# Decoder block on one core: fourteen experts' weights split by GpSimd in the routed stage instead of in the cross-attention, attention scores issued one by one on alternating array halves

## The chip, the core and the metric

One core of a Trainium2 chip. Its engines run their own programs side by side and meet at semaphores: PE (TensorE, matrix products into PSUM), DVE (VectorE), ACT (ScalarE), POOL (GpSimd), and SP (SyncE), which issues DMAs. POOL and ACT issue DMAs as well. The metric is the device time of one launch in microseconds, the median of several runs.

## What is computed

One pre-norm decoder layer on x of (8, 256, 512), with self-attention, cross-attention to a context of the same shape, and a mixture of experts:

```python
x = x + attn(layernorm(x), w_qkv, w_out)                 # 16 heads of 32, causal
x = x + xattn(layernorm(x), ctx, ctx, encoding, Wq, bq, Wk, bk, Wv, bv, Wm, bm)
x = x + moe(layernorm(x), Wg, W1, W3, W2, Ws1, Ws3, Ws2)

# xattn: the 256 positions are channels, the 512 features are the sequence
q, k = rotary(Wq x + bq), rotary(Wk c + bk);  v = Wv c + bv      # 16 heads of 16
scores = einsum('bdhn,bdhm->bhnm', q, k) / sqrt(16)
out = Wm einsum('bhnm,bdhm->bdhn', softmax(scores), v) + bm

# moe: 16 experts of 352 hidden units, 4 of them for each token, and 2 shared ones
h = silu(einsum('td,eid->eti', xt, W1)) * einsum('td,eid->eti', xt, W3)
y = einsum('etd,te->td', einsum('eti,edi->etd', h, W2), combine)
```

## The kernel before

Products of f32 data are made of f16 pairs: a value is split into a high part (the value rounded to f16) and a low part (what is left, rounded to f16), and a product is three f16 matmuls, high x high, high x low and low x high (`split_product`). So every operand has to be split once: the high part by ACT or POOL, the low part by a subtraction on POOL or DVE.

The stages run one after the other: self-attention, cross-attention, then routing with the first shared expert, the routed experts, and last the combination with the second shared expert.

**Cross-attention** (`cross_attention`). It handles eight batches in a pipeline of turns, t = -2 to 8. In turn t the attention of batch t is done (`attend`), the row maxima of batch t+1 (`maxima`), and the projections of batch t+2 (`projects`); pieces of batches t+3 and t-1 are prepared and finished (`pairs`, `ends`). A turn has 16 quads, and every engine's program is written out as a loop over them, so the tests such as `qd in (1, 3, 7, 9)` are the schedule. In a quad PE makes four score tiles of 128x512 (`ca_sc`, in `scores`) whose maxima DVE takes (`maximum`, `ca_mx`), four transposed ones for the next quad (`ca_st`, in `transposed_scores`) that ACT exponentiates (`exponent`, `ca_pt`), and it weighs the values with them (`weigh_values`, `ca_pv`). A score tile has 48 or 49 rows of contraction, and the heads lie in partitions 0 to 63 or 64 to 127, so a tile uses one half of the array's rows. `ca_sc` and `ca_st` have three PSUM banks each (`RING = 3`). One more bank, `ca_proj`, is shared by the projections, the values, the turned maxima and the output; `USERS` lists who has it in which order.

Between the scores, DVE does `swap` and `add` of the rotary embedding, `turn_weighed`, `invert`, `divide` (`ca_quot`) and `turn_back` (`ca_yf`) for each of four groups of heads, `residual`, `keep_values` and `normalise`; ACT does `out` (takes a projection out of PSUM), `high_part`, `y_high_part`, `x_high_part`, `keep_maxima`; POOL does `roll` and the low parts; SP does `spill` and `stack` (the rotated q and k go through DRAM into their stacked form), `load_rows` and `load_context`.

The experts' weights are split here too. From quad 4 on each attending turn has 12 pieces of 704 or 768 columns, two experts' worth: SP loads a piece (`load_piece`), ACT makes the high part (`split_piece`), POOL the low part (`low_piece`), SP stores the pair to DRAM (`store_piece`, `we_pairs`). After eight turns `we_pairs` holds all 16 experts.

**Routed experts** (`routed_experts`). Tokens have been sorted by expert into tiles of 128 rows; PE works through 74 tiles. For a tile it makes the two hidden products (`re_ab`, 24 matmuls), transposes the f16 pair of the hidden values (`re_ht_ps`, `turn_hidden`, which waits for `h_low`), and makes the output (`re_yp`, 9 matmuls, in `output`, which counts `y_done`). The hidden values pass through ACT (`re_gate`), DVE (`re_hf`), ACT (`re_hp`, high part, L1542) and DVE (`re_hp`, low part, L1567, which signals `h_low`). PE's order is `hidden` of tile n+1, `turn_hidden` of n, second half of n+1, `output` of n. Weights have two slots. POOL waits until the last tile of an expert is done and loads the next pair from `we_pairs` into that slot with one DMA of 2176 KB. At the start POOL also loads and splits the second shared expert's weights (`jobs`, L1466 and L1468).

## Time and profile before

| | us |
|---|---|
| median of 3 runs (1991.07 to 1993.84) | 1992.2 |
| the profiled execution: its own time | 1993.37 |
| its span in the trace | 1991.8 |
| cross-attention in it, 481.6 to 1217.0 | 735.4 |
| routed experts in it, 1400.0 to 1856.8 | 456.8 |
| busy in the whole span: PE, DVE, ACT, POOL | 1502.9, 1059.7, 694.4, 575.4 |

How to read what follows. A row of the busy times has a stretch (from and to, in us from the start of the span), its length, then for PE, PE's weight loads (PEld), DVE, ACT and POOL the busy time with the count of instructions, then the granted clock of PE as a share of 2.4 GHz, the share of the DMA engines, and GB/s. A row of the timeline has start and length in us, engine, line, operation, output <- inputs, shapes and count, and in brackets the idle time before it and what ended it. A row of the waits says who waited for whom: total, times, longest. Matmul rows have a pipeline tail in their length: neighbours overlap. Each load of an expert's pair is 2176 KB, 9.2 us from issue to landing at the median; the second shared expert's weights are as large, in two DMAs.

### The profile page before, as it was taken

To read this page: it belongs to the slowest core of one execution; us is meant where nothing else is said; L and a number is where in the kernel's file an instruction comes from. 1 tells how busy PE (TensorE), PEld (TensorE's weight loads), DVE (VectorE), ACT (ScalarE), POOL (GpSimd) and SP (SyncE) were. 2 spreads that over 40 slices of the span, in tenths; PEclk is the share of its full clock that TensorE was granted. 3 is DMA by queue.
4 is the path that set the end of the run, shared out by engine and by line. 5 is a ranking of instruction groups with operands and counts; after the bars stand their busy time and mean duration, and the time that the engine had idled before them with its cause. 6 is when DMAs were issued, how large, how long until landed. Compare 5 with 4: busy or idle time off the path is not lost. (4 is left out here: it accounts for less than half of the span.)

```text
span 1991.8 us, 28978 instructions
## 1 busy us (share of the span) xinstructions
PE 1502.9 (75%) x9512; PEld 687.2 (35%) x9521; DVE 1059.7 (53%) x1809; ACT 694.4 (35%) x1187; POOL 575.4 (29%) x464
## 2 busy tenths in 40 slices
PE   2778787875266667768677774885699999999957
PEld 1344444442011111112111111532366566666423
DVE  6343434346387777876776726851143333333564
ACT  4322221212116766666766683511011111111211
POOL 3000000002534554554544332467200000000462
PEclk9989898987558989898898886787799999999978
DMA  4252516160423555545644451035555645654564
GB/s 169 72 172 61 182 48 195 36 207 31 116 53 96 159 167 147 174 125 147 181 123 135 154 160 70 1 134 204 182 179 179 176 138 176 181 177 137 140 178 131
DMA packets 212442, 273.45 MB, mean 137 GB/s; under 512 B 91984, under 2 KB 159120, under 8 KB 210064
## 3 DMA queue, kind: packets, MB, share of 16 engines
q1 hardware_dynamic: 188880, 181.68, 32.2%
q0 software_dynamic: 12832, 71.44, 10.3%
q10 hardware_dynamic: 10656, 19.40, 2.6%
q8 instruction: 39, 0.64, 0.1%
q14 instruction: 35, 0.29, 0.1%
HBM read 132.29 MB, written 120.06 MB: 127 GB/s over the span
## 5 line engine op out<-in xcount | busy, mean ns | idle before, releaser
L805 DVE TENSOR_REDUCE ca_mx<-ca_sc 128x1 f32<-128x512 f32 x512 | 331.9, 678 | 165.9 <-PE ca_sc L725 163.6
L77 PE MATMUL re_ab<-re_w,re_xt 128*128 x1800 | 297.6, 316 | 42.5 <-DMA re_w<-we_pairs 38.5
L938 ACT ACTIVATE ca_pt<-ca_st 128x512 f32<-128x512 f32 x512 | 274.9, 590 | 37.5 <-PE ca_st L737 37.1
L737 PE MATMUL ca_st<-ca_qs,ca_ks 49*128 49x512 f16 x512 | 110.2, 426 | 155.6 <-ACT ca_pt L938 155.5
L77 PEld LDWEIGHTS re_ab<-re_w,re_xt 128*128 128x128 f16 x1800 | 174.1, 99 | 141.2 <-issue 44.4
L1003 POOL TENSOR_TENSOR ca_wpair<-ca_wraw,ca_wpair 128x704 f16<-128x704 f32 (+1 forms) x96 | 149.3, 1561 | 65.7 <-ACT ca_wpair L895 65.7
L750 PE MATMUL ca_pv<-ca_pt,ca_va 128*32 128x512 f32 x1024 | 163.1, 701 | 0.9 <-DVE ca_turned L818 0.6
L77 PE MATMUL re_yp<-re_w,re_ht 128*128 (+1 forms) x666 | 156.0, 379 | 0.0
L737 PEld LDWEIGHTS ca_st<-ca_qs,ca_ks 49*128 49x128 f16 x512 | 25.3, 94 | 349.6 <-ACT ca_pt L938 287.6
L725 PE MATMUL ca_sc<-ca_ks,ca_qs 48*128 48x512 f16 x512 | 113.1, 438 | 39.5 <-DVE ca_mx L805 20.6
L478 POOL TENSOR_TENSOR sa_yt<-sa_yf,sa_yt 128x512 f16<-128x512 f32 x16 | 18.5, 1156 | 385.0 <-ACT sa_yt L461 385.0
L77 PE MATMUL sh_ab<-fx_xn,sh_pair 128*128 128x512 f16 (+1 forms) x576 | 126.6, 382 | 3.6 <-PEq L1408 3.4
L1540 ACT ACTIVATE re_gate<-re_ab 128x352 f32<-128x352 f32 x75 | 34.8, 463 | 252.8 <-PE re_ab L77 252.8
L1457 POOL DMA_DIRECT2D re_w<-we_pairs x16 | 8.6, 536 | 371.0 <-PE re_yp L77 354.2
L1565 DVE TENSOR_TENSOR re_hf<-re_ab,re_gate 128x352 f32<-128x352 f32 x75 | 39.3, 524 | 112.1 <-PE re_ab L77 112.1
L1576 DVE COPY re_ht<-re_ht_ps 128x768 f16<-128x768 f16 x74 | 41.3, 557 | 108.1 <-PE re_ht_ps L1499 108.1
L77 PE MATMUL sh_yp<-sh_pair,sh_ht 128*128 128x512 f16 (+1 forms) x288 | 72.2, 412 | 34.5 <-DVE x_sb L1208 34.4
L1608 POOL DMA_INDIRECT co_yg<-slot_outs,fx_index x64 | 69.7, 1090 | 96.7 <-POOLq L1408 61.5
L1542 ACT ACTIVATE re_hp<-re_hf 128x352 f16<-128x352 f32 x75 | 37.2, 496 | 173.2 <-DVE re_hf L1565 173.2
L77 PE MATMUL sa_proj<-sa_xn,sa_w 128*128 x384 | 85.3, 385 | 10.7 <-DVEq L407 10.7
L77 PEld LDWEIGHTS re_yp<-re_w,re_ht 128*128 128x128 f16 (+1 forms) x666 | 65.1, 98 | 69.0
L988 POOL TENSOR_TENSOR ca_tf<-ca_tf,ca_freq 128x512 f32<-128x512 f32 x32 | 40.8, 1276 | 162.0 <-DVE ca_rf L796 162.0
(235 smaller groups left out, 2415.9 us busy)
## 6 DMA issues: line engine op xcount, KB each, us to landing
re_w<-we_pairs POOLq DMA_DIRECT2D x16, 2176.0 KB, 9.2
ca_wraw<-in_we SPq DMA_DIRECT2D x64, 352.0 KB, 3.8
we_pairs<-ca_wpair SPq DMA_DIRECT2D x64, 352.0 KB, 2.9
slot_rows<-sa_zeros SPq DMA_DIRECT2D x12, 1792.0 KB, 16.0
slot_outs<-re_ys ACTq DMA_DIRECT2D x74, 256.0 KB, 2.0
ca_wraw<-in_we SPq DMA_DIRECT2D x32, 384.0 KB, 4.8
we_pairs<-ca_wpair SPq DMA_DIRECT2D x32, 384.0 KB, 2.9
sa_scratch<-sa_qk SPq DMA_DIRECT2D x16, 512.0 KB, 4.5
```

Source lines behind the costliest of these rows:

```text
L77: last = nc.tensor.matmul(out, lhs(a, c), rhs(b, c), start=(c == 0 and n == 0), stop=(c == chunks - 1 and n == len(PRODUCTS) - 1))
L725: nc.tensor.matmul(sc[:, (2 * n + a) % RING, :], qs[rows, c % SLOTS, pair, qt * P:(qt + 1) * P], ks[rows, c % SLOTS, pair, :], start=True, ...
L737: nc.tensor.matmul(st[:, (2 * n + a) % RING, :], ks[rows, b % SLOTS, pair, kt * P:(kt + 1) * P], qs[rows, b % SLOTS, pair, :], start=True, ...
L750: last = nc.tensor.matmul(pv[j * 32:(j + 1) * 32, :], va[:, b % 2, kt, h, :], pt[:, (4 * qd + j) % 8, :], start=(kt == 0), stop=(kt == 3), ...
L805: nc.vector.reduce_max(mx[:, qd // 4, qd % 4, 2 * a + jj:2 * a + jj + 1], sc[:, (2 * n + a) % RING, :], AX.X).then_inc(maxed, 1)
L938: nc.scalar.activation(pt[:, (4 * qd + k) % 8, :], st[:, (2 * n + a) % RING, :], ACT.Exp, scale=SCALE).then_inc(exp_done, 1)
L988: nc.gpsimd.tensor_tensor(tf[:, u, :], tf[:, u, :], freq[:, 0, :], ALU.mult).then_inc(rolled, 1)
L1003: nc.gpsimd.tensor_tensor(wpair[:, m % 2, 1, 0:n], wraw[:, m % 3, 0:n], wpair[:, m % 2, 0, 0:n], ALU.subtract).then_inc(w_low, 1)
L1542: nc.scalar.activation(hp[:, s, 0, :], hf[:, s, :], ACT.Copy).then_inc(h_high, 1)
L1565: nc.vector.tensor_tensor(hf[:, s, :], ab[:, s, 1, 0:I], gate[:, s, :], ALU.mult).then_inc(h_ready, 1)
L1576: nc.vector.tensor_copy(ht[:, s, :, :], ht_ps[:, 0:2 * IC, :]).then_inc(ht_ready, 1)
L1608: nc.gpsimd.indirect_dma_start(out=yg[:, m % RING, :], out_offset=None, in_=slot_outs, in_offset=bass.IndirectOffsetOnAxis(ap=route["index ...
```

## The change

Four things change.

- **Pieces.** Only 12 pieces, those of experts 0 and 1, are still split in the cross-attention, in the turn t = -1, which has no exponentials. `we_pairs` has two experts.
- **Routed stage.** Experts 2 to 15 are loaded raw, as f32, into a buffer of two (`raw_w`). When a slot is free POOL splits the expert itself: one `tensor_copy` and one `tensor_tensor` subtraction over all 4352 columns. `w_ready` takes the place of the DMA's semaphore on PE. At the start both stored pairs, the shared expert's two pieces and two raw experts are all issued at once.
- **Scores.** `scores` and `transposed_scores` issued two matmuls on one wait; `score` and `transposed_score` issue one. Their order by halves of the array is k % 2 for the one and 1 - k % 2 for the other. The order of heads in `weigh_values` and in the layout of Wm follows.
- **Places in the schedule.** Several small steps stand in later quads; `turn_maxima(3, b)` goes from quad 1 to 7.

```diff
-            def scores(c, qd, jj):
-                n, pair, qt = 2 * (QUADS * c + qd) + jj, 2 * (qd // 4) + jj, qd % 4
-                if n >= 1:
-                    pe.wait_ge(maxed, 2 * n - 1)
-                for a in range(2):
...
+            def score(c, qd, k):
+                m, pair, qt = 4 * (QUADS * c + qd) + k, 2 * (qd // 4) + k // 2, qd % 4
+                if m >= RING:
+                    pe.wait_ge(maxed, m - RING + 1)
+                rows = slice(64 * (k % 2), 64 * (k % 2) + ROWS)
...
+            def transposed_score(b, qd, k):
+                if m >= RING:
+                    pe.wait_ge(exp_done, m - RING + 1)
+                a = 1 - k % 2
...
@@ DVE turn
-                    if projects and qd in (1, 3, 7, 9):
-                        swap((1, 3, 7, 9).index(qd), e)
+                    if projects and qd in (2, 4, 8, 10):
+                        swap((2, 4, 8, 10).index(qd), e)
-                    if projects and qd in (2, 5, 8, 11):
+                    if projects and qd in (3, 6, 9, 11):
                         add(...)
-                    if pairs and qd == 10:
+                    if pairs and qd == 11:
                         normalise(j, f)
@@ ACT turn
-                    if attend and qd == 2:
+                    if attend and qd == 8:
                         keep_maxima(3, b)
-                    if projects and qd in (3, 6, 9, 12):
+                    if projects and qd in (5, 7, 11, 12):
                         high_part(...)
-                    if attend and qd in (5, 9, 13):
+                    if attend and qd in (6, 10, 14):
                         y_high_part(qd // 4 - 1, b)
-                    if pairs and qd == 11:
+                    if pairs and qd == 13:
                         x_high_part(j, f)
-                    if attend and qd >= FIRST_PIECE:
-                        split_piece(b, qd - FIRST_PIECE)
+                    if t == -1 and qd >= FIRST_PIECE:
+                        split_piece(qd - FIRST_PIECE)
@@ SP turn
-                    if projects and qd in (4, 6, 10, 12):
+                    if projects and qd in (6, 8, 12, 13):
                         spill(...)
-                    if projects and qd in (5, 7, 11, 13):
+                    if projects and qd in (7, 9, 13, 14):
                         stack(...)
@@ routed experts, POOL
-            with pool.Fori(1, E // 2) as i:
-                for k in range(2):
-                    pool.wait_ge(w_loaded, 32 * i + 16 * k)
-                    pool.wait_ge(y_done, done + 2)
-                    load(2 * i + k, k)
+            for e in range(2, E):
+                done = pool.value_load(route["ends"][0:1, e - 2:e - 1], min_val=0, max_val=TILES)
+                pool.wait_ge(y_done, done + 2)
+                pool.sem_inc(w_free, 1)
+                pool.wait_ge(raw_loaded[e % 2], 16 * (e // 2))
+                nc.gpsimd.tensor_copy(w[:, e % 2, 0, :], raw_w[:, e % 2, :]).then_inc(w_high, 1)
+                pool.wait_ge(w_high, e - 1)
+                nc.gpsimd.tensor_tensor(w[:, e % 2, 1, :], raw_w[:, e % 2, :], w[:, e % 2, 0, :], ALU.subtract
+                                        ).then_inc(w_ready, 1)
+                if e + 2 < E:
+                    pool.wait_ge(w_ready, e + 1)
+                    load_raw(e + 2)
```

What stands in a row on POOL at the routed stage. Before, the loop's body, one expert of two:

```order
312 L1473 ISA [waits re_w_loaded]
313 L1473 TENSOR_LOAD fx_ends
314 L1473 ISA x2
315 L1474 REGISTER_ALU
316 L1457 ISA [waits re_y_done]
317 L1457 DMA re_w<-we_pairs 128x8704
```

With the change, the same place, one expert of fourteen (`re_raw_w` is the f32 buffer):

```order
225 L1477 TENSOR_LOAD fx_ends
226 L1477 ISA x2
227 L1478 REGISTER_ALU
228 L1481 CAST re_w<-re_raw_w 128x4352 [waits re_y_done,re_raw_loaded0]
229 L1483 TENSOR_TENSOR re_w<-re_raw_w,re_w 128x4352 [waits re_w_high]
230 L1460 DMA re_raw_w<-in_we 128x4352 [waits re_w_ready]
```

Between the free slot and ready weights there was a DMA; now there are two POOL instructions, and the DMA stands behind them for an expert two later.

PE in the cross-attention, a quad of a full turn (`ca_st` are the transposed scores, `ca_sc` those for the maxima). Before:

```order
525 L737 MATMUL ca_st<-ca_qs,ca_ks 128x512 [waits ca_exp_done]
526 L737 MATMUL ca_st<-ca_qs,ca_ks 128x512
527 L725 MATMUL ca_sc<-ca_ks,ca_qs 128x512 [waits ca_maxed]
528 L725 MATMUL ca_sc<-ca_ks,ca_qs 128x512
529 L737 MATMUL ca_st<-ca_qs,ca_ks 128x512 [waits ca_exp_done]
530 L737 MATMUL ca_st<-ca_qs,ca_ks 128x512
531 L725 MATMUL ca_sc<-ca_ks,ca_qs 128x512 [waits ca_maxed]
532 L725 MATMUL ca_sc<-ca_ks,ca_qs 128x512
```

With the change:

```order
524 L736 MATMUL ca_st<-ca_qs,ca_ks 128x512 [waits ca_exp_done]
525 L724 MATMUL ca_sc<-ca_ks,ca_qs 128x512 [waits ca_maxed]
526 L736 MATMUL ca_st<-ca_qs,ca_ks 128x512 [waits ca_exp_done]
527 L724 MATMUL ca_sc<-ca_ks,ca_qs 128x512 [waits ca_maxed]
528 L736 MATMUL ca_st<-ca_qs,ca_ks 128x512 [waits ca_exp_done]
529 L724 MATMUL ca_sc<-ca_ks,ca_qs 128x512 [waits ca_maxed]
530 L736 MATMUL ca_st<-ca_qs,ca_ks 128x512 [waits ca_exp_done]
531 L724 MATMUL ca_sc<-ca_ks,ca_qs 128x512 [waits ca_maxed]
```

The same eight matmuls stand in turn instead of in pairs, and each waits for itself.

## Rows read from the trace of the kernel before

**Rows 1.** Busy time by stage (columns as told under the profile above).
```profile
481.60:1217.00 735.40, 486.44 (x2752) 125.67 (x2752) 493.32 (x935) 431.39 (x765) 345.13 (x255) 0.82 0.47 135
...
1400.00:1856.80 456.80, 443.08 (x2910) 267.26 (x2910) 171.31 (x299) 71.98 (x150) 22.34 (x22) 0.98 0.56 169
```

**Rows 2.** The same view, turns of the cross-attention: first, six full, seventh, eighth.
```profile
544.00:603.90 59.90, 37.39 (x130) 10.20 (x130) 49.68 (x91) 12.41 (x19) 18.86 (x15) 0.53 0.21 46
...
603.90:1077.80 473.90, 336.79 (x2044) 87.93 (x2042) 350.28 (x666) 315.41 (x568) 245.01 (x182) 0.90 0.53 151
...
1077.80:1147.40 69.60, 52.04 (x318) 13.33 (x318) 49.52 (x95) 46.17 (x84) 23.21 (x16) 0.88 0.40 127
...
1147.40:1200.00 52.60, 38.33 (x204) 8.10 (x208) 12.15 (x22) 42.19 (x76) 21.61 (x15) 0.80 0.47 149
```

**Rows 3.** Who waited for whom, 759.4 to 838.9: total us, times, longest.
```profile
DVE ca_mx L805 <- PE ca_sc L725: 20.4, 15, 3.3
...
PE ca_st L737 <- ACT ca_pt L938: 20.1, 23, 4.1
...
ACT ca_tf L915 <- PE ca_proj L77: 8.3, 4, 3.2
...
ACT ca_yt L927 <- DVE ca_yf L834: 6.5, 3, 3.2
...
ACT ca_xn L899 <- DVE ca_norm L784: 2.2, 1, 2.2
```

**Rows 4.** Groups of instructions, the same turn: busy us, mean ns, idle before.
```profile
L895 ACT ACTIVATE ca_wpair<-ca_wraw 128x704 f16<-128x704 f32 x8 | 6.2, 780 | 0.0
```

**Rows 5.** Timeline of PE, then DVE, cross-attention: start us, length us, what.
```profile
763.22 0.39 PE L737 MATMUL ca_st<-ca_qs,ca_ks 49*128 49x512 f16 x2 [0.27 <-ACT ca_pt L938]
...
768.70 1.47 PE L77 MATMUL ca_proj<-ca_xn,ca_w 128*128 128x512 f16 x6
...
770.10 1.07 PE L750 MATMUL ca_pv<-ca_pt,ca_va 128*32 128x512 f32 x8
...
767.63 1.89 DVE L805 TENSOR_REDUCE ca_mx<-ca_sc 128x1 f32<-128x512 f32 x3 [0.65 <-PE ca_sc L725]
```

**Rows 6.** Timeline of POOL, routed stage.
```profile
1424.74 2.53 POOL L1466 CAST sh_pair<-sh_raw 128x2816 f16<-128x2816 f32 x1 [13.37 <-DMA sh_raw<-in_we]
...
1427.36 5.52 POOL L1468 TENSOR_TENSOR sh_pair<-sh_raw,sh_pair 128x2816 f16<-128x2816 f32 x1
...
1611.19 0.53 POOL L1457 DMA_DIRECT2D re_w<-we_pairs  x1 [28.78 <-PE re_yp L77]
```

**Rows 7.** Timeline of PE, then of DVE, one tile of the routed stage.
```profile
1608.43 2.11 PE L77 MATMUL re_yp<-re_w,re_ht 128*128 x9
...
1616.23 1.96 PE L77 MATMUL re_ab<-re_w,re_xt 128*128 x12
...
1618.03 0.50 PE L1499 MATMUL re_ht_ps<-ident,re_hp 128*128 128x128 f16 x6
...
1615.65 0.53 DVE L1567 TENSOR_TENSOR re_hp<-re_hf,re_hp 128x352 f16<-128x352 f32 x1 [0.56 <-ACT re_hp L1542]
```

**Rows 8.** DVE beside POOL: DVE, POOL, DVE; durations ns min/median/max of one line.
```profile
1227.96 4.26 DVE L122 TENSOR_SCALAR fx_ln_std<-fx_ln_moments 128x16 f32<-128x16 f32 x1
...
1226.69 5.51 POOL L226 TENSOR_TENSOR sh_pair<-sh_raw,sh_pair 128x2816 f16<-128x2816 f32 x1 [6.04 <-ACT sh_pair L220]
...
1433.73 0.93 DVE L1567 TENSOR_TENSOR re_hp<-re_hf,re_hp 128x352 f16<-128x352 f32 x1 [0.56 <-ACT re_hp L1542]
...
L826 DVE TENSOR_TENSOR ca_quot<-ca_turned,ca_rden x32: 401/408/1878, 624.8 to 1203.9; 128x256 f32<-128x256 f32 x32
```

**Rows 9.** Busy time around an idle stretch; timeline of PE after another.
```profile
154.95:161.15 6.20, 0.00 (x1) 0.01 (x1) 4.18 (x3) 2.53 (x3) 2.30 (x2) 0.77 0.00 0
...
161.15:165.10 3.95, 3.95 (x10) 1.44 (x11) 0.00 (x0) 0.01 (x1) 0.00 (x0) 0.50 0.00 0
...
1425.62 3.70 PE L77 MATMUL re_ab<-re_w,re_xt 128*128 x12 [3.87 <-DMA re_xt<-slot_rows]
```

More of the change, by code:

```diff
@@ L551, in cross_attention @@
     WP = 2 * NP
[L554 to L555 removed]
+    USERS = (("project", 2, 0), ("project", 2, 1), ("out", -1, 0), ("out", -1, 1), ("maxima", 1, 0),
+             ("project", 2, 2), ("maxima", 0, 3), ("project", 2, 3), ("maxima", 1, 1), ("values", 1, 0), ("values", 1, 1),
              ("values", 1, 2), ("maxima", 1, 2), ("values", 1, 3))
@@ L728, in transposed_scores @@
-            def transposed_scores(b, qd, jj):
-                n, pair, kt = 2 * (QUADS * b + qd) + jj, 2 * (qd // 4) + jj, qd % 4
-                if kt == 0 and jj == 0:
-                    pe.wait_ge(row_loaded[qd // 4], 32 * (b + 1))
-                if n >= 1:
-                    pe.wait_ge(exp_done, 2 * n - 1)
-                for a in range(2):
-                    rows = slice(64 * a, 64 * a + ROWS + 1)
-                    nc.tensor.matmul(st[:, (2 * n + a) % RING, :], ks[rows, b % SLOTS, pair, kt * P:(kt + 1) * P],
-                                     qs[rows, b % SLOTS, pair, :], start=True, stop=True).then_inc(st_done[a], 1)
+                if m >= RING:
+                    pe.wait_ge(maxed, m - RING + 1)
@@ L1455, in _, with load_raw @@
         def _(pool):
-            def load(e, slot):
-                pool.dma_start(w[:, slot, :, :], we_pairs[e]).then_inc(w_loaded, 16)
-            load(0, 0)
-            pool.wait_ge(w_loaded, 16)
-            load(1, 1)
+            def load_raw(e):
+                pool.dma_start(raw_w[:, e % 2, :], we_dram[e]).then_inc(raw_loaded[e % 2], 16)
+            for e in range(2):
+                pool.dma_start(w[:, e, :, :], we_pairs[e]).then_inc(pairs_loaded[e], 16)
             for dram, raw, _pair in jobs:
                 pool.dma_start(raw, dram).then_inc(jobs_loaded, 16)
+            load_raw(2)
+            load_raw(3)
+            for e in range(2):
+                pool.wait_ge(pairs_loaded[e], 16)
+                pool.sem_inc(w_ready, 1)
             pool.wait_ge(jobs_loaded, 16 * len(jobs))
@@ L1703, in laid_out @@
     wm = np.zeros((4, P, CH), np.float32)
-    order = [2 * g + j // 2 + H // 2 * (j % 2) for g in range(4) for j in range(4)]
+    order = [2 * g + j // 2 + H // 2 * (1 - j % 2) for g in range(4) for j in range(4)]
     wm.reshape(4, 4, 2, XHD, CH)[:, :, 0] = heads(get("L0_xattn_Wm").T).reshape(H, XHD, CH)[order].reshape(4, 4, XHD, CH)
```

122 lines of the change are left out of this document (63 added, 59 removed).

## The prediction

> **What bounds the kernel now.** I read the busy times by stage first [rows 1]. Two stages are touched. The cross-attention takes 735.4 us, with no engine over 67% busy (DVE 493.3, PE 486.4). The routed experts take 456.8 us, with PE busy for 443.1 of them at a granted clock of 0.98: that stage is bound by PE, and a stall of PE there goes straight into the time. Both stages lie one after the other on the one path, so gains and losses add.
>
> Inside the cross-attention I read the turns [rows 2]. The turn of maxima alone takes 59.9 us, six full turns together 473.9 us (79.0 each), then one without projections 69.6 and one of attention alone 52.6. In a full turn DVE is busy for 58.4 us, ACT for 52.6, PE for 56.1 (a sixth of the row), of 79.0. The waits of one of them, 759.4 to 838.9 [rows 3], say why nobody is full: DVE waits 20.4 us for scores of PE, PE waits 20.1 us for exponentials of ACT, and ACT waits 8.3 us for a projection and 6.5 and 2.2 us for products of DVE (turned values, normalised rows) that it takes in too early a place. It is a ring of three engines in program order, with three PSUM banks between each two. The end of a stall is mostly ACT's.
>
> **The change part by part: cross-attention.** (1) ACT loses 12 splits in each of eight attending turns. Their row gives 0.78 us for the 704-column form [rows 4] (768 columns a little more), so about 0.80 us: 12 x 0.80 = 9.6 us a turn. POOL loses twelve subtractions, which were beside other work, except where they held DVE (below). SP loses 24 DMAs a turn. Twelve splits come into the turn of maxima alone, where ACT is idle by four fifths: no cost. SP's `spill` and `stack` there now stand behind `store_piece`, as they did in every full turn before.
> (2) Scores are issued singly. Before, a pair starts together (x2 in one row of 0.39 us, two matmuls on two halves of the array [rows 5]) and needs two free banks of three, so one exponential or maximum is left in flight as PE fires. Now each needs one bank, and two are left. A `ca_mx` takes 0.68 us alone and 0.60 more for each that follows at once (three in 1.89 us [rows 5]); a pair costs at least 0.68 + 0.39 + two wake-ups of 0.06, so 1.2 us, against 1.2 for two maxima, with nothing over for delay. Singly, PE has 1.2 us of cover. The order of halves (1,0,0,1) still puts one `st` and one `sc` on different halves, so PE pays nothing if both are ready, and at most 0.2 us for each of 64 pairs where they aren't; that time lies in PE's idle 20 us.
> (3) `y_high_part` and `x_high_part` go one and two quads later behind DVE's part: most of 6.5 + 2.2 us of ACT's waits goes. The wait for projections, 8.3 us, stays.
> What is late next: DVE. I add up its work by quads: 64 maxima x 0.60 = 38.2, four groups of turn, invert, divide, turn back x 2.1 = 8.3, swaps and adds 5.6, the rest 5.4: 57.5 us, and this is the floor of a full turn. PE's stretches without scores still starve it: after the last score of a quad three maxima (1.8 us) are queued, while PE does a projection (1.4 from start to start), the weighing of values (1.07 with its tail, so some 0.9) and a new score (0.5) [rows 5]: 1.0 us short, four times; an output projection has 12 matmuls in place of 6, 2.4 short, twice; the values product has six of half the width, 0.3 short, four times: 10 us. With 2.5 us for what ACT and the half clock (granted 0.90) still bring: 70 us a turn. Bounds: 63 (DVE 91% busy), and 77: if I take for each quad the greatest of three engines' loads and add them, before gives 63.0 and after 60.7, only 2.3 less, so 77 follows if all 16 us of bubbles stay. I take 70, since single issue and later places attack the bubbles themselves.
> So six turns: 473.9 - 420 = 54 us; the turn without projections 69.6 to 61 (9); attention alone 52.6 to 45 (7.6 of its 9.6 us of splits); maxima alone 59.9 to 54 (6; DVE busy 49.7). Together **77 us gained** (25 to 110).
> (4) `stack` of the last unit moves to quad 14, behind `load_rows`. It must land before the next turn's first score. It was two quads early; with shorter turns it is nearly due: 0 to 2 us a turn, in the range.
>
> **Routed stage.** (5) For each of 14 experts POOL now waits for the free slot and then does one CAST and one subtraction of 128x4352, single instructions. Rates [rows 6]: CAST 2.53 us for 2816 columns, so 3.9 for 4352; subtraction 5.52 for 2816, so 8.5. Slots come free as before, 0.65 us ahead of the old DMA issue at 1611.19, that is at the end of `re_yp` at 1610.54 [rows 6, 7]. If POOL were alone this is hidden: the weights are ready 12.8 us after, and two issues of the old load are 28.78 + 0.53 = 29.3 us apart [rows 6], five tiles of 5.86; the shortest experts have four tiles, 23.4 us, less the 3.9 that PE is ahead.
> But POOL isn't alone. DVE operations that read two operands from SBUF, and this one `tensor_scalar`, don't run beside a POOL instruction: they stand until it ends [rows 8]. The 16-column `fx_ln_std` took 4.26 us and ended (1232.22) with POOL's subtraction (1226.69 + 5.51 = 1232.20); `ca_quot`, 0.408 at the median, took up to 1.878. In the routed stage `re_hp<-re_hf,re_hp` (0.53 us) took 0.93 the one time that a CAST ran (1433.73; CAST over at 1434.28). It is of this kind, and PE's transposes wait for it each tile.
> Now the clock of one tile [rows 7]: slot free at 1610.54, CAST from 1610.8 to 1614.7, subtraction from 1614.8 to 1623.3. The low part of the next tile is due at 1615.65, 0.9 us after the subtraction has begun. It stands until 1623.3, ends 1623.6, and the transposes, at 1618.03 before, begin at 1623.8: **5.8 us of stall on PE**, once for each expert: 14 x 5.8 = 81 us. Bounds 5.0 and 6.5, by 0.7 us either way in POOL's two operations.
> (6) The clock. After an idle stretch of 6.20 us PE had half speed for 3.95 us of work more [rows 9]: 2.0 us lost. After 3.87 us idle, 12 matmuls took 3.70 us, against 1.96 at full speed [rows 7, 9]: 1.7 us lost there alone, and with the transposes and the 12 matmuls behind them some 2.9 at most. For stalls of 5.8 I take 2.3: 14 x 2.3 = 32 us (1.0 to 2.9 each).
> (7) At the start two pairs of weights, the shared expert and two raw experts, 11 MB, are queued at once; before, 6.6 MB. The tile's transposing DMA landed only once that queue was dry: PE waited 3.87 us [rows 9]. Some 4 us more (0 to 6). The first expert's load is still first in its queue.
> Routed stage: **+117 us** (84 to 138).
>
> By the Trainium skill (SBUF — State Buffer, "SBUF: two separate sides") the port pair that VectorE and GpSimd share is "an exclusive lock", held "for the whole instruction". The trace agrees, up to 5.5 us of a POOL instruction; no row here shows 8.5. By its page GPSIMD Engine Reference, section 3.1 (Elementwise), a two-input operation costs about 2.6 cycles an element at 1.2 GHz: an estimate of 9.4 us for 4352 columns, where the row's rate gives 8.5; by the page each stall would be 0.9 us longer and the sum 13 us higher. The row decides.
>
> **The sum.** The profiled execution took 1993.4 us (span 1991.8 and 1.6 around it), 1.2 above the median of 1992.2, and I sum against it: 1993.4 - 77 + 81 + 32 + 4 = 2033.4; less the 1.2 to the median, **2032 us**, 2.0% slower.
>
> **The rivals.** A, faster: the low part isn't held, or it slips in between CAST and subtraction. For it: only 0.9 us part the CAST's end from the low part's arrival; if the CAST starts or runs 1 us later, DVE goes first, the subtraction then ends near 1625, and the low part of the tile after (due 1621.5, slack 1.85) costs 1 to 2 us. Then the routed stage loses 14 x 0 to 1.5 + 4, and the time is 1992 - 77 + 14 = **1929** (1915 to 1940). Against it: CAST's rate was measured in this stage, and every expert meets POOL in the same phase, since POOL starts at the tile's own end. Chance 0.14.
> B: the ring of three engines keeps its bubbles, and a turn falls to 77 only. For it: the sum by quads, 63.0 against 60.7. Then 1992 - 25 + 117 = **2084**. Chance 0.12.
> C: DVE is filled to its floor, 62 to 63 us a turn and the others likewise (-115), with short stalls (14 x 6.5 = 91) and no more at the start: 1992 - 115 + 91 = **1968**. For it: the three waits are all attacked at once. Against: the turn of maxima alone, with no ACT in it, reached 83% of DVE. Chance 0.12.
> D: `stack` lands late, 3 us on each of seven turns: 2032 + 21 = **2053**. Chance 0.06.
> The change turns from gain to loss where stalls in the routed stage exceed 77 / 14 = 5.5 us an expert; forecast 8.1 with the clock.
>
> **How the numbers follow.** The forecast (2000 to 2062) has 0.56. I leave out A (0.14) and a little above B, and take 1964 to 2086. A difference under 0.2% (4 us) can't be told from none. Faster: A, C and a few of the forecast's tail: 0.27. Same: 0.04. Slower: 0.69.
>
> **What would show it.** In the routed stage: 14 rows of `re_hp` on DVE at some 8 us, each ending with POOL's subtraction; a wait PE `re_ht_ps` <- DVE `re_hp` of about 81 us in all; clock near 0.85. In the cross-attention: full turns of 70 us, PE's wait for exponentials well under 20 us a turn, DVE over 80% busy. I am wrong if `re_hp` stays at 0.53 us, or if the turns stay near 77.

## The result, and the profile after

The changed kernel takes **2023.7 us** (median of 4 runs, 2021.5 to 2028.1). The kernel before, run beside it, takes 1991.6 us. The ratio is 1.016 (95% interval 1.014 to 1.018): it is slower by 1.6%, or 32 us. Another set of runs gave 1.017 (1.014 to 1.020). The profiled execution has a span of 2022.2 us at a mean granted clock of 0.87.

The two stages moved in opposite directions. The cross-attention ends at 1126.7 us where it ended at 1216.1, 89 us earlier. The routed stage, from its first product to the first gather behind it, takes 570.2 us where it took 451.1, 119 us longer. Here are the busy times of the stretches that answer to [rows 1, 2], same columns (start:end, length, busy us and count of PE, weight load, DVE, ACT, POOL, granted clock, DMA share, GB/s): the turn of maxima alone, two full turns, the turn of maxima and exponentials without projections, the turn of attention alone, and the routed stage.

```profile
545.90:607.80 61.90, 48.77 (x130) 12.37 (x129) 50.66 (x92) 21.09 (x31) 37.84 (x27) 0.50 0.59 170
...
675.30:743.60 68.30, 57.42 (x345) 16.98 (x344) 59.27 (x114) 43.25 (x84) 23.86 (x19) 0.95 0.22 47
743.60:811.80 68.20, 57.31 (x345) 16.94 (x344) 59.19 (x113) 43.15 (x84) 23.85 (x19) 0.95 0.22 47
1013.20:1068.20 55.00, 46.26 (x304) 13.73 (x305) 46.58 (x90) 34.45 (x68) 4.63 (x4) 1.00 0.00 1
1068.20:1112.10 43.90, 36.32 (x220) 9.11 (x218) 12.57 (x25) 34.42 (x69) 4.61 (x4) 1.00 0.00 1
```
```profile
1321.70:1892.00 570.30, 477.67 (x2912) 280.54 (x2913) 271.28 (x302) 71.96 (x150) 190.29 (x44) 0.90 0.44 130
```

The third full turn, whose waits stand in [rows 3], fell from 79.5 to 68.3 us (the mean of all six from 79.0 to 67.6), and DVE is now busy for 87% of it. In the routed stage PE has the same 2,900 matmuls as before, but they take 477.7 us and not 443.1, DVE's 302 operations take 271 us and not 171, and the clock is 0.90 and not 0.98. The waits of a full turn answer to [rows 3] (who waited for whom: us in all, times, longest):

```profile
ACT ca_pt L937 <- PE ca_st L736: 14.0, 8, 4.7
...
DVE ca_mx L804 <- PE ca_sc L724: 9.0, 9, 2.2
...
ACT ca_tf L914 <- PE ca_proj L77: 6.1, 4, 1.7
...
PE ca_st L736 <- ACT ca_pt L937: 3.4, 10, 0.6
```

PE's wait for exponentials went from 20.1 to 3.4 us, DVE's wait for scores from 20.4 to 9.0. ACT now waits for PE instead. The routed stage tells the other half. First its waits, then one expert's stall in the timelines of PE, DVE and POOL (start us, length us, what, and in brackets the idle time before it and what ended it); these answer to [rows 6, 7].

```profile
PE re_ht_ps L1510 <- DVE re_hp L1578: 73.8, 14, 5.3
```
```profile
1541.22 3.81 POOL L1481 CAST re_w<-re_raw_w 128x4352 f16<-128x4352 f32 x1 [24.12 <-PE re_yp L77]
...
1545.11 8.42 POOL L1483 TENSOR_TENSOR re_w<-re_raw_w,re_w 128x4352 f16<-128x4352 f32 x1
1546.16 7.75 DVE L1578 TENSOR_TENSOR re_hp<-re_hf,re_hp 128x352 f16<-128x352 f32 x1 [0.56 <-ACT re_hp L1553]
```
```profile
1546.75 1.96 PE L77 MATMUL re_ab<-re_w,re_xt 128*128 x12
1553.97 0.82 PE L1510 MATMUL re_ht_ps<-ident,re_hp 128*128 128x128 f16 x6 [5.27 <-DVE re_hp L1578]
1554.59 3.73 PE L77 MATMUL re_ab<-re_w,re_xt 128*128 x12
```

POOL's subtraction starts at 1545.11 and ends at 1553.53. DVE's low part asks 1.05 us after its start, stands until it is over, and lasts 7.75 us in place of 0.53. PE waits 5.27 us for it and then runs at half the full clock (granted 0.50 from 1554.0 to 1558.1): 12 matmuls take 3.73 us and not 1.96. This happens 14 times, once for each expert. The last loss is at the start of the stage, where [rows 9] had 3.87:

```profile
1343.70 3.70 PE L77 MATMUL re_ab<-re_w,re_xt 128*128 x12 [15.45 <-DMA re_xt<-slot_rows]
```

### The profile page after: what moved, and what is told of

It reads as the page before. It is cut to its first block and busy times, and to the rows that moved or that the text cites. A ratio compares the mean times of both kernels' runs of the same rounds, so it can differ in the third digit from the quotient of the medians.

```text
span 2022.2 us, 28535 instructions
## 1 busy us (share of the span) xinstructions
PE 1548.3 (77%) x9520; PEld 715.4 (35%) x9521; DVE 1156.4 (57%) x1809; ACT 624.8 (31%) x1103; POOL 619.3 (31%) x407
## 5 line engine op out<-in xcount | busy, mean ns | idle before, releaser
L77 PE MATMUL re_ab<-re_w,re_xt 128*128 x1800 | 321.0, 333 | 55.4 <-POOLq L1470 40.0
L937 ACT ACTIVATE ca_pt<-ca_st 128x512 f32<-128x512 f32 x512 | 264.5, 596 | 101.1 <-PE ca_st L736 101.1
L724 PE MATMUL ca_sc<-ca_ks,ca_qs 48*128 48x512 f16 x512 | 190.9, 427 | 50.2 <-DVE ca_mx L804 29.0
L736 PE MATMUL ca_st<-ca_qs,ca_ks 49*128 49x512 f16 x512 | 172.4, 400 | 41.1 <-ACT ca_pt L937 35.1
L1578 DVE TENSOR_TENSOR re_hp<-re_hf,re_hp 128x352 f16<-128x352 f32 x75 | 140.6, 1875 | 42.1 <-ACT re_hp L1553 42.1
L749 PE MATMUL ca_pv<-ca_pt,ca_va 128*32 128x512 f32 x1024 | 148.6, 645 | 1.0 <-DVE ca_turned L817 0.5
L1481 POOL CAST re_w<-re_raw_w 128x4352 f16<-128x4352 f32 x14 | 53.3, 3809 | 306.4 <-PE re_yp L77 306.4
L736 PEld LDWEIGHTS ca_st<-ca_qs,ca_ks 49*128 49x128 f16 x512 | 42.2, 95 | 236.4 <-ACT ca_pt L937 148.8
L1483 POOL TENSOR_TENSOR re_w<-re_raw_w,re_w 128x4352 f16<-128x4352 f32 x14 | 117.9, 8419 | 1.2
L1510 PE MATMUL re_ht_ps<-ident,re_hp 128*128 128x128 f16 (+1 forms) x444 | 41.7, 238 | 73.8 <-DVE re_hp L1578 73.8
```

Of the source, the lines that this page charges most:

```text
L77: last = nc.tensor.matmul(out, lhs(a, c), rhs(b, c), start=(c == 0 and n == 0), stop=(c == chunks - 1 and n == len(PRODUCTS) - 1))
L724: nc.tensor.matmul(sc[:, m % RING, :], qs[rows, c % SLOTS, pair, qt * P:(qt + 1) * P], ks[rows, c % SLOTS, pair, :], start=True, stop=True ...
L736: nc.tensor.matmul(st[:, m % RING, :], ks[rows, b % SLOTS, pair, kt * P:(kt + 1) * P], qs[rows, b % SLOTS, pair, :], start=True, stop=True ...
L749: last = nc.tensor.matmul(pv[j * 32:(j + 1) * 32, :], va[:, b % 2, kt, h, :], pt[:, (4 * qd + j) % 8, :], start=(kt == 0), stop=(kt == 3), ...
L937: nc.scalar.activation(pt[:, (4 * qd + k) % 8, :], st[:, m % RING, :], ACT.Exp, scale=SCALE).then_inc(exp_done, 1)
L1481: nc.gpsimd.tensor_copy(w[:, e % 2, 0, :], raw_w[:, e % 2, :]).then_inc(w_high, 1)
```

## Experiments

Twelve runs in three sets of four, each set beside the kernel before. `s_raw_late`, `r_load_waits`, `r_loads4` and `f_all` ran on a second chip, on which the kernel before took 2030.5 us: the stage between the cross-attention and the routed one, which no kernel here changes, lasted some 222 us and not 195. I therefore compare ratios, and lengths of the two stages from the traces. Those 27 us don't account for all of the 38.7 that the kernel before lost on the second chip, and no trace of it there tells where the other 12 went; so these four ratios can make their kernels look up to 0.006 better than they are, and where ratio and stage length disagree the length is the safer. A time "on the first chip" below is a ratio times 1991.8 us, an estimate. "Full turn" is the third of six (759.4 to 838.9 before), "routed" is first routed product to first gather.

| kernel | splits in cross-attention | scores, places | routed stage | ratio (95%) | full turn | routed |
|---|---|---|---|---|---|---|
| before | 16 experts | pairs, old | loads pairs | 1 | 79.5 | 451.1 |
| e_splits_out | 2 | pairs, old | loads pairs | 0.971 (0.967-0.975) | 70.7 | 452.0 |
| g_single_only | 2 | single, old | loads pairs | 0.950 (0.949-0.952) | 65.1 | 452.7 |
| c_routed_as_before | 2 | single, new | loads pairs | 0.958 (0.956-0.960) | 68.3 | 451.7 |
| d_schedule_only | 16 | single, new | loads pairs | 0.982 (0.980-0.984) | 75.1 | 451.1 |
| after | 2 | single, new | one subtraction | 1.016 (1.014-1.018) | 68.3 | 570.2 |
| r_phase | 2 | single, new | one, with a wait | 1.016 (1.014-1.017) | 68.3 | 570.6 |
| s_raw_late | 2 | single, new | one, raw loads later | 1.010 (1.007-1.013) | 70.6 | 564.3 |
| r_pieces8 | 2 | single, new | 8 pieces | 0.992 (0.989-0.995) | 68.3 | 525.1 |
| r_load_waits | 2 | single, new | 8 pieces, load waits | 0.961 (0.957-0.965) | 68.3 | 465.2 |
| r_loads4 | 2 | single, new | 4 pieces, 4 loads | 0.963 (0.958-0.968) | 68.3 | 464.9 |
| f_all | 2 | single, new | that, raw loads later | 0.960 (0.956-0.964) | 68.3 | 469.3 |
| f_best | 2 | single, new | 4 and 4, start as before | 0.960 (0.957-0.963) | 68.3 | 453.4 |

### The cross-attention alone

`c_routed_as_before` has the whole new cross-attention and the old routed stage. Its loop of loads and their count are those of before, but it reads one of two finished pairs:

```
-                pool.dma_start(w[:, slot, :, :], we_pairs[e]).then_inc(w_loaded, 16)
+                pool.dma_start(w[:, slot, :, :], we_pairs[slot]).then_inc(w_loaded, 16)
```

> The changed kernel's whole cross-attention (splits of experts 0 and 1 alone, single issue, its places), with the routed stage of before: it loads finished pairs, only that every even expert gets expert 0's pair and every odd one expert 1's (the output is left wrong by that; tiles, transfers and products are the same in number and size). Theory T (the change is a gain of 89 us in the cross-attention and a loss of about 119 us that GpSimd's two long instructions and the start of the routed stage make): 1992 - 89 = 1903, from 1896 to 1910; cross-attention ends near 1127, routed stage 451 long, PE stalls on re_hp none. Rival (part of the loss behind the cross-attention comes from elsewhere: later placed work, code, clock): over 1912.

Measured: 1906.5 us, ratio 0.958, where 1903 was expected. The cross-attention ends at 1126.0 and the routed stage takes 451.7. So the gain of 85 us is real and stands alone, and all of the loss (1.016 less 0.958, 116 us) lies in the routed stage. Three kernels take the gain apart. `e_splits_out` leaves out the splits of fourteen experts only, on ScalarE as shown and in the same way on GpSimd (their subtractions) and SyncE (their transfers):

```
-                    if attend and qd >= FIRST_PIECE:
+                    if t == -1 and qd >= FIRST_PIECE:
```

> The kernel before with one edit: only experts 0 and 1 are split (in the turn of maxima alone), pair issue and all places as before, routed stage reads these two pairs for all experts (output left wrong by that). Theory 1 (ScalarE's 12 splits a turn are most of the gain: 9.6 us a turn over seven turns, 60 to 67): 1925 to 1940. Theory 2 (the pair issue bounds the turn, ScalarE's time is beside it): 1970 to 1990. Rival 3 (splits alone give the whole 89): 1903.

Measured: 1930.6 us (0.971), a full turn of 70.7. The splits were worth 58 to 61 us, those of ScalarE together with GpSimd's subtractions, which went with them. That the second part counts is seen in DVE, which loses no work here and is yet busy for 55.6 us of the third full turn and not 58.9. One of its groups, before and in `e_splits_out`:

```profile
L784 DVE TENSOR_SCALAR ca_norm<-x_sb,ca_mean,ca_rstd 128x512 f32<-128x512 f32 x2 | 2.2, 1157 | 0.0
```
```profile
L784 DVE TENSOR_SCALAR ca_norm<-x_sb,ca_mean,ca_rstd 128x512 f32<-128x512 f32 x2 | 1.0, 540 | 0.0
```

How the 8.8 us of the turn divide between ScalarE's time and DVE's being held was not tested. `d_schedule_only` does the rest without that: single issue and new places, all sixteen experts split as before.

> The changed kernel's single issue and places, but all 16 experts split in the eight attending turns as before, routed stage as before (computes the reference). Theory 1 (splits are most of the gain, ScalarE still bounds the turn here): 1965 to 1985, turns 75 to 78. Theory 2 (the pair issue bounded): 1915 to 1935, turns near 70. That the two parts add up would be e's and this one's gains together 89; if they overlap or need each other the sum is off by over 10.

Measured: 1955.1 us (0.982), between my two theories; a full turn of 75.1. The two gains, 58 and 36 us by the ratios, sum to 94, and both together give 84: they overlap a little. `g_single_only` then adds single issue to `e_splits_out` and leaves the places as they were.

> e_splits_out (splits of experts 0 and 1 alone, pair issue, places of before: 0.971 of before) with single issue on alternating halves, and not the new places; routed stage as in e_splits_out, experts 0 and 1's pairs for all (output left wrong by that). c_routed_as_before differs from it by the places alone (0.958). Theory P (with the splits gone, single issue is worth little by itself, and the new places of swaps, outputs and y parts give most of the last 1.3 %): 0.967 to 0.972, full turns 69 to 71. Theory I (single issue gives it): 0.957 to 0.961, full turns 68 to 69.

Measured: **1894.1 us, ratio 0.950, better than either theory allowed**, and 12 to 16 us better than `c_routed_as_before` (by medians and by ratios), which differs by the places alone. Single issue is worth 5.6 us a full turn (70.7 to 65.1), and the new places **cost** 3.2 (65.1 to 68.3). They give some back in the turn of maxima alone (66.9 to 61.4) and in the one without projections (57.2 to 55.0), and the cross-attention ends 11 us later. Both turns have the same operations. DVE's groups show where the 3.2 us are, first with the new places, then with the old (busy us, mean ns | idle before):

```profile
L825 DVE TENSOR_TENSOR ca_quot<-ca_turned,ca_rden 128x256 f32<-128x256 f32 x4 | 2.5, 630 | 0.0
L783 DVE TENSOR_SCALAR ca_norm<-x_sb,ca_mean,ca_rstd 128x512 f32<-128x512 f32 x2 | 1.8, 952 | 0.0
...
L813 DVE TENSOR_SCALAR ca_nm<-ca_nmf 128x16 f16<-128x16 f32 x4 | 1.6, 392 | 0.0
...
L809 DVE TENSOR_SCALAR ca_nmf<-ca_mx 128x16 f32<-128x16 f32 x4 | 1.3, 323 | 0.0
```
```profile
L825 DVE TENSOR_TENSOR ca_quot<-ca_turned,ca_rden 128x256 f32<-128x256 f32 x4 | 1.6, 405 | 0.0
...
L783 DVE TENSOR_SCALAR ca_norm<-x_sb,ca_mean,ca_rstd 128x512 f32<-128x512 f32 x2 | 1.0, 538 | 0.0
...
L809 DVE TENSOR_SCALAR ca_nmf<-ca_mx 128x16 f32<-128x16 f32 x4 | 0.7, 173 | 0.0
L813 DVE TENSOR_SCALAR ca_nm<-ca_nmf 128x16 f16<-128x16 f32 x4 | 0.6, 159 | 0.0
```

The four groups take 7.2 us and not 3.9: 3.3 us of being held, against a turn that is 3.2 longer. In the timeline of `c_routed_as_before` the pair is seen directly, POOL first, then DVE:

```profile
793.97 1.33 POOL L992 TENSOR_TENSOR ca_qk<-ca_tf,ca_qk 128x512 f16<-128x512 f32 x1 [1.29 <-ACT ca_qk L920]
796.44 2.26 POOL L979 TENSOR_TENSOR ca_xn<-ca_norm,ca_xn 128x512 f16<-128x512 f32 x2 [1.14 <-ACT ca_xn L898]
```
```profile
793.75 1.83 DVE L783 TENSOR_SCALAR ca_norm<-x_sb,ca_mean,ca_rstd 128x512 f32<-128x512 f32 x2
...
796.73 0.89 DVE L809 TENSOR_SCALAR ca_nmf<-ca_mx 128x16 f32<-128x16 f32 x1
```

The first `ca_norm` started ahead of POOL's low part at 793.97 and took 0.53 us; the second met it and took 1.37. The 16-column `ca_nmf`, asked for at 796.73, ends at 797.62, when the first of POOL's two operations from 796.44 is over. The new places put DVE's products of SBUF operands where POOL has its own. That this makes all of the 3.2 us is by sums; I moved no single place alone.

### The routed stage: what holds DVE

`r_pieces8` changes only the number of instructions of the subtraction:

```
-                nc.gpsimd.tensor_tensor(w[:, e % 2, 1, :], raw_w[:, e % 2, :], w[:, e % 2, 0, :], ALU.subtract
-                                        ).then_inc(w_ready, 1)
+                for m in range(8):
+                    at = slice(m * WC // 8, (m + 1) * WC // 8)
+                    last = nc.gpsimd.tensor_tensor(w[:, e % 2, 1, at], raw_w[:, e % 2, at], w[:, e % 2, 0, at],
+                                                   ALU.subtract)
+                last.then_inc(w_ready, 1)
```

> The changed kernel with one edit: GpSimd's subtraction of each of the 14 experts in 8 instructions of 544 columns instead of one of 4352 (cast whole as before). Theory T (VectorE's low part waits until GpSimd's running instruction ends, then gets in): the hold falls from 5.3 us to at most one piece, about 1.1; stalls 14 x 0 to 1.1 = 0 to 15, half clock gone with them, so 2023.7 - 74 - 40 + 8 = 1918, range 1908 to 1935. Rival L (VectorE is held as long as GpSimd has subtraction work queued, pieces or not, or it is the SBUF traffic that slows it): 2015 to 2030. Rival C (the cast holds just as well and takes the subtraction's place): 1955 to 1985, low parts of about 3 us.

Measured: 1978.7 us (0.992), where I expected 1918. The hold behaved as expected, and the sum did not come out. DVE's low part, over its 75 instances (ns min/median/max), first after the change, then in eight pieces:

```profile
L1578 DVE TENSOR_TENSOR re_hp<-re_hf,re_hp x75: 525/526/7762, 1329.4 to 1887.2; 128x352 f16<-128x352 f32 x75
```
```profile
L1584 DVE TENSOR_TENSOR re_hp<-re_hf,re_hp x75: 525/526/1367, 1331.0 to 1843.6; 128x352 f16<-128x352 f32 x75
```

The longest is 1.37 us, POOL's pieces take 1.27 us each on the mean, and PE has no wait on `re_hp` left. POOL's subtractions last longer than with one instruction (10.0 us an expert and not 8.4), so neither its busy time nor its traffic held DVE, but the length of the instruction that is running. Yet another wait came up. First the sum of PE's waits in the stage (the start's 15.4 among them), then one of them in the timeline:

```profile
PE re_ab L77 <- DMA re_xt<-slot_rows: 56.7, 12, 15.4
```
```profile
1524.21 3.26 PE L77 MATMUL re_ab<-re_w,re_xt 128*128 x12 [4.27 <-DMA re_xt<-slot_rows]
```

Against `c_routed_as_before` the stage is 73 us longer: 52 us more of these waits, and 21.5 us more of PE's busy time at half clock behind them (465.1 and 443.6). In the trace a token tile's transposing load lands 3.3 us after its issue at the median. The load that was issued at 1512.33 landed at 1523.89, 11.6 us later. The raw weights (2176 KB, 10.5 us on the way) had been issued at 1510.86, 1.5 us ahead of it:

```profile
1510.86 0.54 POOL L1460 DMA_DIRECT2D re_raw_w<-in_we  x1 [0.30 <-POOL re_w L1488]
```

With two token buffers and 5.86 us a tile, a load has 7.6 us. After the change, the stalled PE and DVE had kept the two apart: the raw load started after the long hold, when the next token load was still 4.7 us off (1553.83 and 1558.51). Before, too, the pair was loaded 3.5 us ahead of a token load (1611.19 and 1614.64), which took 6.6 us and just fitted. Two kernels test this. `r_load_waits` leaves everything as in `r_pieces8` and starts each raw load behind a token load, not ahead of it:

```
+                    pool.wait_ge(ab_done, done + 4)
+                    pool.sem_inc(w_free, 1)
                     load_raw(e + 2)
```

> r_pieces8 with one edit: after an expert's subtraction GpSimd waits until the token load of the next tile but one is let go (the wait on ab_done), and then loads the next raw weights; same transfers, same sizes, a few us later. Theory Q (r_pieces8 lost its gain because each raw load of 10.5 us is issued 1.5 us ahead of a token load that is then 11.6 us on the way and not 3.2, eleven stalls of about 4 us): those stalls go, 2 tiles in flight cover it; 1978.7 - 41 - 16 (half clock) = 1922, range 1916 to 1932, low parts of the hidden units still about 0.5 us. Rival B (16 transfer engines or the SBUF are short whenever a raw load runs, wherever it starts): 1965 to 1980.

Measured: ratio 0.961, which is 1914 us on the first chip, against 0.992: 62 us for a later start of twelve transfers of the same size, and 60 us by the lengths of the stage. The stage's waits on `re_xt` are now the start and three of under 1 us:

```profile
PE re_ab L77 <- DMA re_xt<-slot_rows: 17.5, 4, 15.5
```

Rival B, a stage that stays slow wherever the load starts, is out. The two transfers still slow each other, though: each of the twelve token loads now has the raw load 0.4 us behind it and takes 6.9 to 8.3 us, not 3.3. That is just within its 7.6 us, and the three that took longer than 7.6 are the three waits. What the later start bought is about 4 us a load, and that was enough. `r_loads4` cuts both, the subtraction into four instructions and the raw load into four quarters, each issued when its quarter is subtracted:

```
+                for m in range(LOADS):
+                    last = m == LOADS - 1
+                    nc.gpsimd.tensor_tensor(w[:, e % 2, 1, cut(m)], raw_w[:, e % 2, cut(m)], w[:, e % 2, 0, cut(m)],
+                                            ALU.subtract).then_inc(w_ready if last else w_part, 1)
...
+                        load_raw(e + 2, m)
```

> The changed kernel with the subtraction in 4 instructions of 1088 columns, and each quarter of the next raw weights loaded as soon as its quarter is subtracted (cast whole). Theory T and Q together (hold at most one instruction of about 2.2 us, of which about 1.9 is slack; a token load is behind at most one or two quarters of 2.6 us): no stall on re_hp over 0.5, none on re_xt but the start: 1918 to 1935, most likely 1924. Rival (the hold is not per instruction, or four queued quarters act as one load): 1970 to 2020.

Measured: 0.963, or 1918 us on the first chip. The subtractions take 2.27 us each. Most held low parts last 1.6 to 2.0 us in place of 0.53, within PE's slack of 1.9 us; the longest, 2.63, uses up all of it, and there is no wait on `re_hp` among PE's. Behind the start's 10.3 us, six short waits on `re_xt` stay, 5.8 us in all and 1.8 at most:

```profile
PE re_ab L77 <- DMA re_xt<-slot_rows: 16.1, 7, 10.3
```

`r_phase` was meant to put the long subtraction just behind a low part. It did not test that.

> The changed kernel with one wait more: GpSimd starts each whole subtraction just behind VectorE's low part of the same tile (wait on h_low). Theory T and Q: the next low part is asked for 5.3 us later and held 3.1 us, of which 1.9 is slack: stall 1.2 an expert (17 in all) where it was 5.3; but the raw load then falls just ahead of a token load, as in r_pieces8, for about 2.9 us an expert (32) and half clock behind both. Ratio to before 0.985 to 1.000. Rival (the time goes with GpSimd's busy time, wherever it starts): 1.014 to 1.020. Rival (hold gone altogether and token loads in time): 0.962 to 0.968.

```
                 pool.wait_ge(w_high, e - 1)
+                pool.wait_ge(h_low, done + 1)
```

Measured: 1.016, as the changed kernel. The condition was one tile off. The low part that it waits for ended at 1541.2, before the cast began, so the subtraction started 0.16 us behind the cast and the next low part fell into it again:

```profile
1541.58 3.81 POOL L1481 CAST re_w<-re_raw_w 128x4352 f16<-128x4352 f32 x1 [24.05 <-PE re_yp L77]
1545.55 8.42 POOL L1484 TENSOR_TENSOR re_w<-re_raw_w,re_w 128x4352 f16<-128x4352 f32 x1 [0.16 <-POOL re_w L1481]
```

The right condition, one tile on, could stand still for an expert with one tile. What a better phase would give stays untried. `after_again` is the changed kernel beside it.

> The changed kernel itself, beside the three others on the same chip: 1.014 to 1.018 of before, 14 stalls of 5.3 us on re_hp, one gap of 10 to 15 us on re_xt at the start.

Measured: 2027.4 us, ratio 1.017, 14 stalls of 5.3 us and 15.3 us at the start.

### The start of the routed stage

After the change six loads are under way at once: two pairs, two parts of the shared expert, two raw experts. The second token load was issued at 1313.17 and landed at 1343.38, 0.2 us behind the last raw load. Only the two pairs had been issued ahead of it; the other four followed within 1.8 us, and it was held by them as well. `s_raw_late` waits for both first token tiles before it loads raw weights:

```
             pool.wait_ge(jobs_loaded, 16 * len(jobs))
+            for s in range(2):
+                pool.wait_ge(x_loaded[s], 16)
+            load_raw(2)
+            load_raw(3)
```

> The changed kernel with one edit: at the start of the routed stage the raw weights of experts 2 and 3 are loaded only once the first two token tiles have landed. Theory S (the second transposing load of tokens, issued at 1313.17, landed at 1343.38 because the 4.5 MB of raw weights stood in the transfer engines ahead of it): the one gap of 15.4 us on re_xt falls to about 4 (before: 3.9), and the half clock behind it goes: 2023.7 - 11.6 - 4 = 2008, range 2003 to 2014; the 14 stalls of 5.27 stay. Rival (the shared expert's raw weights and the two pairs, which before loads as well, hold it): 2018 to 2026.

Measured: 1.010 and not 1.016; the interval (1.007 to 1.013) reaches from 6 to 19 us of gain, and the expected 1.008 lies within it. The trace says less than I expected: the gap of 15.45 became one of 6.24 and one of 2.35, because the shared expert's weights still hold the second token load (issued at 1350.70, 0.2 and 0.7 us ahead of their two loads, it landed at 1370.12, 0.5 us behind the later of them), and the raw loads now meet the fourth. So the raw loads held 7 to 9 us of the 11.6, and the stage is 5.9 us shorter. `f_all` joins this to `r_loads4` and adds a third buffer for the stored pairs in the turn of maxima alone.

> r_loads4 plus the late raw loads at the start (s_raw_late) plus a third buffer for the stored pairs in the turn of maxima alone, where ScalarE waited 18.7 us for stores. If the three effects add: 1924 - 15.6 (start) - 3 to 8 (turn of maxima alone 62.0 to 54-59) = 1900 to 1906, range 1896 to 1915; the routed stage is then as long as that of before (445 to 455). If the start's wait only moves to the shared expert's weights: 1910 to 1925.

Measured: 0.960, or 1912 us on the first chip. That is above the 1900 to 1906 of effects that add, and within the 1910 to 1925 of a start whose wait only moves. Its two additions brought nothing that can be told from `r_loads4`. In the trace its routed stage is even 4.4 us longer (469.3 and 464.9): the start's wait on `re_xt` fell from 10.3 to 5.0 us, but a low part then took 5.5 us behind the shared expert's whole subtraction (3.0 us of wait on PE), and the later waits on `re_xt` sum to 11.4 us and not 5.8. The third buffer removed ScalarE's 18.7 us of waits for stores in the turn of maxima alone, yet that turn takes 61.7 us, as without it; in `d_schedule_only`, which has no split in it, it takes 57.4. The two traces show where these 4.3 us are. DVE waits as long for scores (19.5 and 19.6 us), but is busy for 53.7 us and not 49.5, and most of that is one group, in `f_all`, then in `d_schedule_only`:

```profile
L799 DVE TENSOR_TENSOR ca_tf<-ca_tf,ca_rf 128x512 f32<-128x512 f32 x4 | 5.8, 1438 | 0.0
```
```profile
L799 DVE TENSOR_TENSOR ca_tf<-ca_tf,ca_rf 128x512 f32<-128x512 f32 x4 | 2.7, 682 | 0.0
```

So with the third buffer the splits cost that turn what DVE is held by their subtractions on GpSimd; this is again by sums. In the changed kernel DVE is busy for 50.7 us there, and the rest is waiting. `f_best` has `r_loads4`'s pieces and brings the start into the order of before, as shown; expert 2's raw quarters follow the shared expert's weights, and expert 3's its splits, whose subtractions are halved:

```
             for e in range(2):
                 pool.dma_start(w[:, e, :, :], we_pairs[e]).then_inc(pairs_loaded[e], 16)
+                pool.wait_ge(pairs_loaded[e], 16)
+                pool.sem_inc(w_ready, 1)
```

> r_loads4 with another start of the routed stage: pair 0, its landing, pair 1, its landing (as before did for pair 0), the shared expert's weights, then expert 2's raw quarters, the shared expert's splits with their subtractions in halves, then expert 3's raw quarters. Expected: the start's gap on re_xt falls from 10 to 15 us to about 4, as before the change, nothing else moves: ratio 0.955 to 0.960, where r_loads4 had 0.963 and f_all 0.960; the routed stage 452 to 460 long. If the transfers at the start only change their order and the sum of them holds a token tile as long: 0.962 to 0.966.

Measured: **1909.8 us, ratio 0.960 (0.957 to 0.963)**, at the edge of what was expected. It is faster than the kernel before by 82 us and than the changed one by 114 to 118. `f_all` has the same ratio, but on the second chip; by the stage's length `f_best` is 16 us ahead of it. In the trace the stage is nearly that of before, all of POOL's work in it:

```profile
1320.30:1773.70 453.40, 444.06 (x2912) 266.85 (x2913) 208.29 (x302) 72.00 (x150) 225.50 (x136) 0.99 0.64 164
```
```profile
PE re_ab L77 <- DMA re_xt<-slot_rows: 4.6, 4, 3.5
...
PE re_ht_ps L1524 <- DVE re_hp L1592: 0.2, 1, 0.2
```

POOL is busy for 225 us, 35 more than after the change, PE waits 0.2 us for DVE, and the clock is 0.99. The old places of `g_single_only` (0.950) with this routed stage should do better still; that was not run.

## Why the prediction was right, and where its terms were off

The forecast was 2032 and the result 2023.7. The direction was right, and in the routed stage the mechanism and every place too. In the cross-attention the sum of the gain was near, but two of its parts were wrong in sign: the new places cost time in a full turn, and the turn of maxima alone got longer. The gain came out 12 us larger than forecast and the loss 3 us larger, in which 7 us less of stalls and 10 us more for the clock and the start nearly cancel; that the forecast was only 8 us off is in part luck.

- **Step 5, the held low part, was right.** It forecast stalls of 5.8 us, bounds 5.0 to 6.5, 81 in all. They are 5.27 each, 73.8 in all. Cast and subtraction took 3.81 and 8.42 where 3.9 and 8.5 stood, and the low part asked 1.05 us after the subtraction's start, not 0.9. All 14 have the same phase, so rival A (it slips in) didn't occur in any. What the prediction drew on from the Trainium skill (SBUF — State Buffer, "SBUF: two separate sides": the shared port pair is an exclusive lock for the whole instruction) is shown here for an instruction of 8.42 us, which held the low part for 7.2, and `r_pieces8` bears out "whole instruction": the longest hold fell with the piece. By the 2.6 cycles an element of the Trainium skill (GPSIMD Engine Reference, section 3.1, Elementwise) the subtraction would have taken 9.4 us, an estimate; the run shows 8.42.
- **Step 6, the clock, was right.** 32 us were forecast. PE's busy time in the stage rose from 443.1 to 477.7, 34.6 us. In `f_best`, without the stalls, it is 444.1. The sign that was named for it, a clock near 0.85 in the stage, was too low: it is 0.90.
- **Step 7, the start, was mis-sized.** 4 us, at most 6, were forecast. The wait rose from 3.87 to 15.45, 11.6 us. The step gave no working for how much of the extra 4.4 MB would be hidden; nearly none was, as the last raw load landed at 1343.17, 10.9 us behind the shared expert's weights (1332.32). It said that the first expert's load is first in its queue, which was so, but the tile that was late was the second, whose transposing load landed behind all six transfers though four of them were issued after it. `s_raw_late` shows that most of it, not all, is the raw loads.
- **Step 1, ScalarE's splits,** forecast 9.6 us a turn of relief. Taken out alone, with GpSimd's subtractions (`e_splits_out`), they give 8.8 of the full turn. In the same turn DVE's busy time fell by 3.3 us; the step named that DVE had been held there, but put no number on it, so the 8.8 is not ScalarE's relief alone.
- **Steps 2 and 3, issue and places,** were taken together as an attack on bubbles. Their net, 2.4 us a full turn, hides a gain of 5.6 by single issue and a loss of 3.2 by the places. The prediction put no cost on later places and expected of them most of 8.7 us of ScalarE's waits. It had the rule for held DVE operations, but worked it out in numbers for the routed stage only; for the new places it did not ask beside which POOL operation each moved product would fall.
- **The turns.** Full turns: 70 forecast, 67.6 found on the mean of six. Without projections: 61 and 55.0. Attention alone: 45 and 43.9. Maxima alone: 54 forecast, 61.9 found; it got longer, where "no cost" was put on twelve splits in it, because ACT is idle there; ACT was, but DVE is held by their subtractions and ACT waits for stores. Together 77 us were forecast and the cross-attention ends 89.4 earlier. Rival B (turns of 77) is out, and `g_single_only` (65.1) comes within 2 to 3 us of rival C's floor of 62 to 63.
- **Step 4 and rival D** (a late stack) did not occur: no wait for a stacked row stands among a full turn's waits, and the second to fifth full turns agree within 0.1 us.

The sum with the measured terms is 1993.4 - 89.4 + 73.8 + 34.6 + 11.6 = 2024.0; the profiled execution took 2023.9. With 89.4 in place of 77 the change turns at 6.4 us an expert, not 5.5; each expert lost 8.5 (119 / 14, the start included), and with pieces it loses next to nothing.

## What to carry to other kernels

Work on GpSimd beside a busy VectorE is paid for by the length of one instruction, not by its sum: cut it into pieces about as long as the slack of what VectorE has to deliver (here 1.9 us, with pieces of 2.27 or 1.27), and the same work is hidden. Then look at what the removed stall had kept apart. Here a 10 us load now fell 1.5 us ahead of a small one with 7.6 us to spare, and over half of what the pieces could bring was lost (a ratio of 0.992 and not 0.961) until the large one was cut or moved. A change that bundles several edits should be taken apart even where its net is a gain: one of three here was a loss.

## What the runs showed of the hardware

- VectorE's operations from SBUF to SBUF were held not only with two SBUF tensors as operands, but also as `tensor_scalar`: `ca_norm` took 0.54 us alone and 1.37 beside GpSimd, a 16-column `ca_nmf` 0.13 and 0.89 (`c_routed_as_before`). Maxima that read PSUM (0.68) and the stream transposes (0.70) had the same length in both kernels.
- A small transposing load on SP's queue, 3.3 us at the median, took 11.6 us when 2176 KB from GpSimd's queue were issued 1.5 us ahead of it, 6.6 us when issued 3.5 us ahead, and still 6.9 to 8.3 us when issued 0.4 us behind it (`r_load_waits`). In the routed stage of all these traces none landed while a load of weights that had been issued ahead of it was still under way. At the start one took 30.2 us, though only two of the six large loads that it landed behind were issued ahead of it.
- Eight subtractions of 544 columns took 1.27 us each, 10.0 in a row, where one of 4352 took 8.42: about 0.2 us for each further instruction, beside a VectorE that also gets in between them.
